# A Mamba-style block with routed experts: the skip terms move from VectorE to ScalarE

## What is computed

```python
h = quantised_table[x]                                   # (64, 128, 192)
zxbcdt = layernorm(h) @ in_proj_w.T                      # z 384, x 384, B 128, C 128, dt 6
dt = softplus(zxbcdt[..., -6:] + dt_bias)
xBC = silu(causal_conv4(zxbcdt[..., 384:1024], conv_w) + conv_b)
x, Bm, Cm = split(xBC)                                   # x: 6 heads of 64
y = ssd(x * dt, dt * A, Bm, Cm) + D[:, None] * x         # D[:, None] * x: the skip terms
y = y * silu(z)
y = y * rsqrt(mean(y * y) + eps) * norm_w
h = h + sigmoid(gate1) * (y @ out_proj_w.T) + layernorm(h)
```

## Time and profile before

| | us |
|---|---|
| median of 3 runs | 1077.2 |
| lowest and highest | 1069.45, 1078.46 |
| the profiled execution | 1081.81 |
| its span, first to last instruction | 1080.0 |
| its mean granted TensorE clock | 0.928 |

### The profile page before, as it was taken

The page is one execution under the profiler, slowest core; times in us unless marked ns, Lnnn a source line. Parts: engine busy times, 40 slices in busy tenths (PEclk is TensorE's granted clock), DMA queues, the critical chain, the costliest instruction groups (busy, mean ns, idle before and its releaser), DMA issues.

```text
span 1080.0 us, 18795 instructions
## 1 busy us (share of the span) xinstructions
PE 936.5 (87%) x5730; PEld 624.0 (58%) x5731; DVE 648.5 (60%) x2080; ACT 570.5 (53%) x1165; POOL 552.5 (51%) x735
## 2 busy tenths in 40 slices
PE   2688999999998999989999788989798787979995
PEld 2233555544554555545556666768576565858774
DVE  3678999899797998888895236777121111112211
ACT  2677888777776797777862422323223222323230
POOL 6234545557366564663524463334565656664543
PEclk9898999999899999998997769999798988989987
DMA  4910011101010101100101121235221211122211
GB/s 98 325 44 16 11 35 46 46 16 44 32 47 18 44 32 45 47 17 30 33 30 61 50 78 45 80 100 150 68 72 47 57 53 47 51 52 77 68 50 28
DMA packets 50178, 61.90 MB, mean 57 GB/s; under 512 B 22668, under 2 KB 41832, under 8 KB 49556
## 3 DMA queue, kind: packets, MB, share of 16 engines
q0 software_dynamic: 16704, 30.54, 10.1%
q1 hardware_dynamic: 28724, 24.91, 7.7%
q10 hardware_dynamic: 4640, 5.13, 1.6%
HBM read 36.22 MB, written 25.92 MB: 58 GB/s over the span
## 4 chain that ended last, share of the span: by engine, by line
PE 48%; DVE 24%; issue 11%; another core or an unknown queue 5%; ACT 5%; POOL 2%; DMA 2%; DVEq 1%; POOLq 0%; ACTq 0%
DVE xbc L1569 7%; PE cx L1320 6%; PE yb L1320 5%; PE mm L1165 5%; PE mm L1298 4%; PE mm L1291 4%; PE mm L1169 3%; PE sg L1291 3%; PE tp L1132 3%; PE misc L1180 3%; PE sg L1083 3%; PE yb L1114 2%; DVE mix L1590 2%; DVE ybuf L1603 2%
## 5 line engine op out<-in xcount | busy, mean ns | idle before, releaser
L1569 DVE SCALAR_TENSOR_TENSOR xbc<-mm,cw,xbc 128x508 f32<-128x508 f32 (+2 forms) x231 | 167.2, 735 | 26.6 <-ACT xbc L819 22.1
L997 ACT ACTIVATE ht<-mm,b1s 128x256 f32<-128x256 f32 x102 | 44.7, 472 | 250.1 <-PE sg L1291 126.3
L701 POOL DMA_INDIRECT out_dram<-osb,ids_s x80 | 81.9, 1024 | 139.2 <-DVE osb L1998 124.3
L1165 PE MATMUL mm<-xt_a,win_a 128*128 128x512 f32 x248 | 139.7, 656 | 11.3 <-DVE xbc L1569 10.7
L1998 DVE TENSOR_TENSOR osb<-cx,res 128x192 f32<-128x192 f32 x40 | 14.3, 356 | 193.4 <-remote 110.4
L558 POOL TENSOR_TENSOR ybuf<-ybuf,zs 128x384 f32<-128x384 f32 x64 | 64.9, 1015 | 116.1 <-DVE ybuf L1603 114.2
L682 POOL DMA_INDIRECT xg<-hr_dram,ids x80 | 79.3, 992 | 46.2 <-issue 24.3
L1291 PE MATMUL mm<-fx_a,w1a_t 128*128 128x256 f32 x240 | 81.6, 423 | 20.8 <-issue 20.7
L1320 PE MATMUL cx<-w2s,ht 128*128 x408 | 81.5, 349 | 14.1 <-issue 14.1
L1320 PE MATMUL yb<-w2s,ht 128*128 x408 | 80.4, 348 | 3.7 <-issue 3.6
L804 ACT ACTIVATE dec<-sg 128x384 f32<-128x384 f32 x128 | 55.8, 488 | 49.3 <-PE sg L1083 43.3
(11 more groups left out here) (305 smaller groups left out, 2107.2 us busy)
## 6 DMA issues: line engine op xcount, KB each, us to landing
hr_dram<-hr SPq DMA_DIRECT2D x16, 768.0 KB
w2s<-in_w2c_dram SPq DMA_DIRECT2D x4, 576.0 KB
w2s_u<-in_w2u_dram ACTq DMA_DIRECT2D x4, 576.0 KB
list_c<-fill SPq DMA_DIRECT2D x2, 1032.0 KB, 12.2
list_u<-fill SPq DMA_DIRECT2D x2, 1032.0 KB, 18.2
w1a<-in_w1c_dram SPq DMA_DIRECT2D x4, 384.0 KB
w1a_u<-in_w1u_dram ACTq DMA_DIRECT2D x4, 384.0 KB
xg<-hr_dram,ids POOLq DMA_INDIRECT x80
```

Of the source, the lines that this page charges most:

```text
L701: nc.gpsimd.indirect_dma_start(out=out_rows, out_offset=bass.IndirectOffsetOnAxis(ap=ids_s[:, v, t, 0:1], axis=0), in_=osb[:, v, t, :], in ...
L1165: mmul(tile_bank(g2, m)[:, :], win_a[:, column(m):column(m) + P], xt_a[:, p, :], start=True, stop=False)
L1569: ins = stt(out=dst_[:, :, back:L], in0=src[:, :, 0:L - back], scalar=cw[:, m, TAPS - 1 - back:TAPS - back], in1=dst_[:, :, back:L], op0=A ...
```

## The change

ScalarE gets a new last step of its turn, `skip_terms`: three activations of 128 x 512 that write D times x of group g2 into ybuf. It waits for the output product of group g2 - 2 (s_o) and for its own silu (s_xbc), and gives a new semaphore s_skip. VectorE's `y(j)` becomes one addition in place of three multiply-adds, ybuf + yb over all three tiles (128 x 384); for j = 2, which is called for one tile at a time, it stays three instructions of 128 x 128, now additions. Its wait for s_o in `y(0)` becomes a wait for s_skip.

```diff
+        s_skip = sem("skip_terms")
...
+                def skip_terms():
+
+                    if g2 is None:
+                        return
+                    p = g2 % 2
+                    wait(act, s_o, 2 * (g2 - 1))
+                    act.wait_ge(s_xbc, g2 + 1)
+                    for c in range(ZT):
+                        last = nc.scalar.activation(ybuf[:, p, c, :], xbc[:, p, c, :], ACT.Identity, scale=dskip[:, c:c + 1])
+                    last.then_inc(s_skip, 1)
+
...
                 silu_z()
                 from_tp(1)
+                skip_terms()
...
                     if tiles[0] == 0:
                         if j == 0:
-                            wait(dve, s_o, 2 * (g3 - 1))
+                            dve.wait_ge(s_skip, g3 + 1)
                         dve.wait_ge(s_yp, GS * g3 + j + 1)
-                    for c in tiles:
-                        last = stt(out=ybuf[:, p, c, js], in0=xbc[:, p, c, js], scalar=dskip[:, c:c + 1],
-                                   in1=yb[:, c * P:(c + 1) * P], op0=ALU.mult, op1=ALU.add)
+                    c0, c1 = tiles[0], tiles[-1] + 1
+                    last = tt(ybuf[:, p, c0:c1, js], ybuf[:, p, c0:c1, js],
+                              yb[:, c0 * P:c1 * P].rearrange("p (c t) -> p c t", c=c1 - c0), ALU.add)
                     if tiles[-1] == ZT - 1:
                         last.then_inc(s_yd, 1)
```

## The result

The changed kernel takes 1116.6 us (median of 4 runs, 1113.0 to 1118.2) where the kernel before, beside it, takes 1077.8 (1069.5 to 1081.5): ratio 1.036, 95% interval 1.032 to 1.039. It is slower by 39 us, as forecast in sign, but the forecast was 27 us more than before and the range ended at 1113. The profiled execution has a span of 1115.7 us and a mean granted TensorE clock of 0.899, where before it was 0.928.

A forecast was written before the change was run, and what follows sets the result against it. ScalarE's chain, through the exp of sequence 0, was taken as long as VectorE's. Lateness of 27.2 us less 0.6 of VectorE's saving gave 26.6, so 1077.2 became 1104 us; range 1088 to 1113.

The forecast's parts named there:

- The price of the three activations: ScalarE's new step, before the table load and exp of sequence 0: 1.90 us a turn, bounds 1.6 and 2.3.
- The place: At about 15 turn boundaries VectorE's mix waits for ScalarE's exp, 30 us in all; TensorE's seg(1) waits about 1.8 us.
- The last boundary and stage B: Turn 17 has 4 us of cover before x * dt, so loses nothing; stage B keeps its length.
- VectorE's y: VectorE's single addition over 384 columns, claimed to take 0.54 us.
- its saving stays beside the path: VectorE saves 1.0 us a turn, but only 0.6 us in all counts, at the end; bounds 0 and 1.2.
- Rival (a): VectorE bounds stage A and covers ScalarE's addition, so 16 us are saved: 1061 us; 5 in 100.
- The loss: Late exp of sequence 0 at 15 of 16 boundaries, 1.90 us each, 13 with 0.1 spare: 27.2 us.
- rival (c): TensorE's "issue" stops in stage A's side products vanish, returning 7.3 us: 1097 us; 12 in 100.
- The prediction's own signs of being wrong: The mix doesn't wait, the period grows by less than 1 us, or "issue" stops shrink in the side products.
- The spare of 0.1 us: Room the exp of sequence 0 has at a turn boundary before delaying VectorE's mix or TensorE's seg(1).

The follow-up runs named there:

- after_third: The changed kernel unaltered, run again beside the kernel before (1079.0 us) and versions with idle TensorE products: 1120.4 us, ratio 1.039.
- behind_start1: The changed kernel with ScalarE's three activations moved behind start(1) of the next turn, for group g3: 1071.0 us, 0.993 of the kernel before.

## Why the prediction was right and wrong

Right, by its own steps. The price of the three activations: 1.90 us forecast, 1.95 in a row, 715 ns each. The place: VectorE's mix waits at 15 boundaries for 32.0 us in all (30 forecast), TensorE's seg(1) at 15, 2.06 us at all but one (1.8 forecast). The last boundary and stage B lose nothing: from the last table load to the end it is 1115.7 - 597.4 = 518.3 us, before 519.8. VectorE's y: 542 ns (0.54 forecast). That its saving stays beside the path behind the late exp is borne out only in part: by the times it is worth 3.5 to 12.7 us. Rival (a), VectorE as the bound, is out.

Wrong, the step "The loss". It priced TensorE's wait as lateness only, "15 x 1.90 - 13 x 0.1 = 27.2 us", and wrote down seg(1)'s wait of 1.8 us without asking what standing idle does to TensorE's own speed. Its two halves, by the set with after_third:

- The lateness is worth 16 us, not 27. The rest, 11 us, returned in the side products: the effect of rival (c), with 12 in 100, is what happened in sets of this kind, and larger than its 7.3 us; the cause it gives is not shown. The prediction's own signs of being wrong came true: the stops marked "issue" shrank, from 19 with 7.3 us to 2 with 0.7 us, and full-clock turns grew by less than 1 us. In the faster kind of set the 27 us nearly stood: with the stops filled the loss is 1024.7 - 999.4 = 25 us.
- The clock is worth 16 to 26 us, and no case of the prediction had it. The signs were in the trace of before: stage A ran at 0.97 with the granted clock at 1.00 in the turns read closely, and the two longest periods between table loads, 38.0 and 35.3 us, had a fall. The prediction doesn't name the granted clock.

A small reading was off too. The spare of 0.1 us holds for VectorE: at the boundaries of the changed kernel the mix starts 0.11 us after the exp's end. TensorE's seg(1) starts 0.14 to 0.15 us after it when it is plainly waiting, which is all that it had before as well, so it had nothing to spare.

The Trainium skill (TensorE: Matmul & The Clock Gate, section Part 1: The HAM clock gate) says that a monitor throttles TensorE's clock by how busy it has been. The trace agrees in so far: of the twelve falls in the changed kernel's stage A, eleven begin within 2 us of the end of a stop of 2.06 us at a boundary (the granted clock read in steps of 1 us), and most go when the stops are filled with products.

VectorE's saving was also put too low for a kernel without ScalarE's step: "nothing of it is on the path", 0.6 us, bounds 0 and 1.2, but alone it is worth some 10 us. By which wait it reaches the end stays open, since the kernel before has no trace in a set of the faster kind; in the slower kind behind_start1 shows a part of it in the turns with prefixes.

## What to carry over

Where several engines arrive together, read each row of slack as the price of putting work there: the same 1.95 us of ScalarE cost 32 to 41 us ahead of the exp and nothing 3.4 us later, behind start(1). And a wait of TensorE has two prices, the lateness that it hands on and the clock that it may lose behind it; read the granted clock by turns before pricing one, and test it by filling the wait with idle products.

## What the runs showed of the hardware

- TensorE's granted clock fell to the lower level behind stops of 2.06 us in a stage in which it was busy for 92% of the time. Not every stop brought a fall. The clock fell less where stops of 0.9 us were left, and with all stops filled no more than in the kernel before: half-clock time 51 and 20 us.
- More work on TensorE made a kernel 16 to 26 us faster.
- The same kernel takes 1000 us in some sets and 1069 to 1079 in others, even on a chip of the same number, and the effects differ too: the ratio with filled stops is 1.025 in the faster kind and 1.016 in the slower. The cause stays open.
